# An adaLN transformer block on one core: four modulation sections as split 8-row matmuls, a new order around the first batch, and the last batch by tiles of tokens

## The reference

```python
mod = (silu(c) @ wmod).reshape(4, 6, 1, 512)             # c: 4 x 512, wmod: 512 x 3072
sa, ca, ga, sb, cb, gb = (mod[:, i] for i in range(6))
ga = (2 * (ga >= 0) - 1) * maximum(abs(ga), 0.25)        # gb alike
h = layernorm(x) * (1 + ca) + sa
x = x + ga * attention(h, Wqkv, bqkv, Wo, bo)            # softmax(q k' / sqrt(128)) v Wo + bo
h = layernorm(x) * (1 + cb) + sb
# ffn: h W_up' + sum over the top-1 expert e of (h A_e') B_e'
x = x + gb * ffn(h, W_up, gate_w, expert_bias, lora_A, lora_B)
```

## Time and profile before

| | |
|---|---|
| time, median of 3 runs | 217.23 us (216.91 to 218.76) |
| profiled execution: its time, its span | 216.85 us, 215.1 us |
| TensorE busy | 202.5 us, 94% of the span |
| VectorE, ScalarE, GpSimd busy | 130.4, 85.2, 79.1 us |
| TensorE's mean granted clock | 0.929 of full speed |
| moved by DMA | 19.50 MB |

### The profile page before, as it was taken

The page is one execution under the profiler, slowest core; times in us unless marked ns, Lnnn a source line. Parts: engine busy times, 40 slices in busy tenths (PEclk is TensorE's granted clock), DMA queues, the critical chain, the costliest instruction groups (busy, mean ns, idle before and its releaser), DMA issues.

```text
span 215.1 us, 3039 instructions
## 1 busy us (share of the span) xinstructions
PE 202.5 (94%) x1087; PEld 171.1 (80%) x1087; DVE 130.4 (61%) x309; ACT 85.2 (40%) x152; POOL 79.1 (37%) x103
## 2 busy tenths in 40 slices
PE   7999996989999999999999999999999999939992
PEld 6898975878899997798788879888887987726881
DVE  3828043778597561768786567738666365944353
ACT  2142003491177302973454667322466611343010
POOL 3451100008745059004346990004695001580040
PEclk9988997699996955999999999999999999985999
DMA  5999663227005005022002230000221000121004
GB/s 180 368 345 396 155 196 104 95 67 227 0 3 195 0 5 195 0 70 78 5 2 98 105 90 3 0 0 3 98 111 35 0 3 2 38 93 65 0 34 164
DMA packets 12887, 19.50 MB, mean 91 GB/s; under 512 B 3352, under 2 KB 3864, under 8 KB 12872
## 3 DMA queue, kind: packets, MB, share of 16 engines
q1 hardware_dynamic: 12872, 19.31, 26.8%
HBM read 15.09 MB, written 4.21 MB: 90 GB/s over the span
## 4 chain that ended last, share of the span: by engine, by line
PE 44%; POOL 2%; DVE 2%; issue 1%; ACT 1%; POOLq 0%
PE bank L331 30%; PE bank L488 2%; PE bank L486 2%; PE bank L438 2%; PE bank L465 2%; PE bank L525 1%; POOL xs L1246 1%; PE bank L498 1%; PE bank L420 1%; PE bank L417 1%; PE bank L423 1%; PE bank L394 1%; POOL rstd L1231 1%; PE bank L507 1%; PE bank L430 0%
## 5 line engine op out<-in xcount | busy, mean ns | idle before, releaser
L331 PE MATMUL bank<-wup_lo,h2hi 128*128 128x512 f32 x64 | 26.5, 415 | 0.0
L1231 POOL TENSOR_TENSOR rstd<-var_eps,neg_half 128x1 f32<-128x1 f32 x16 | 8.8, 549 | 45.4 <-DVE var_eps L1017 45.4
L331 PE MATMUL bank<-wup_hi,h2hi 128*128 128x512 f32 x64 | 25.4, 397 | 0.0
L331 PE MATMUL bank<-wup_hi,h2lo 128*128 128x512 f32 x64 | 25.4, 397 | 0.0
L741 ACT ACTIVATE xn_p<-xs,shift,rstd 128x512 f32<-128x512 f32 x16 | 13.0, 815 | 31.0 <-POOL shift L1234 31.0
L1246 POOL TENSOR_TENSOR xs<-xs,f_gb 128x512 f32<-128x512 f32 x14 | 17.9, 1289 | 14.8 <-DVE f_gb L1065 14.8
L1223 POOL TENSOR_TENSOR xs<-xs,gabo 128x512 f32<-128x512 f32 x16 | 20.1, 1289 | 0.0
L331 PE MATMUL bank<-h1lo,wqkv_hi 128*128 128x512 f32 x48 | 19.8, 412 | 0.0
L1210 POOL TENSOR_TENSOR wo_ga<-wo_raw,ga_bc 128x512 f32<-128x512 f32 x4 | 5.2, 1292 | 39.4 <-DMA ga_bc<-gates_dram 39.4
L331 PE MATMUL bank<-h1hi,wqkv_lo 128*128 128x512 f32 x48 | 19.0, 396 | 0.0
L331 PE MATMUL bank<-h1hi,wqkv_hi 128*128 128x512 f32 x48 | 19.0, 395 | 0.0
(11 more groups left out here) (164 smaller groups left out, 443.7 us busy)
## 6 DMA issues: line engine op xcount, KB each, us to landing
out_dram<-xs SPq DMA_DIRECT2D x16, 256.0 KB, 2.0
xs<-in_L_attn_x_dram SPq DMA_DIRECT2D x3, 1024.0 KB, 5.3
xs<-in_L_wmod_dram SPq DMA_DIRECT2D x3, 1024.0 KB, 5.2
xs<-in_L_attn_x_dram SPq DMA_DIRECT2D x4, 256.0 KB, 3.4
stage<-in_L_wmod_dram SPq DMA_DIRECT2D x4, 256.0 KB, 4.9
xs<-in_L_wmod_dram SPq DMA_DIRECT2D x4, 256.0 KB, 5.7
stage<-in_L_wmod_dram SPq DMA_DIRECT2D x1, 1024.0 KB, 13.2
ga_bc<-gates_dram SPq DMA_DIRECT2D x4, 256.0 KB, 3.9
```

Of the source, the lines that this page charges most:

```text
L331: mm = nc.tensor.matmul(dst, w, m, start=first and i == 0, stop=last and i == total - 1)
L1231: nc.gpsimd.tensor_tensor(rstd[:, 1, t:t + 1], var_eps[:, 1, t:t + 1], neg_half[:, 0:1], ALU.pow).then_inc(S["ln2_rstd"], 1)
```

## The change

Sections ga, sb, cb and gb (`ROWS`) are made by `mod_rows`: silu(c) is split in two parts of four columns, together the weights of 8 columns, and the section's high and low parts are streamed, 512 columns at a time, in 8 matmuls; the result is 8 rows. ScalarE splits off the high parts (`mod_high`), GpSimd the low ones (`mod_low`), but VectorE those of k = 1 and 3 of cb. ScalarE brings the rows out of PSUM (`mod_row_evacuate`), four small transposes (`mod_columns`) turn them into columns, and a reduction on VectorE (`section`) adds the two parts. Sections ca and sa keep the old form.

The order changes: ca's matmuls stand further ahead between the first transposes; the shift of q and k (`qkv_shift_columns`), the gate's and LoRA's transposes and sb's section stand earlier, `p_transposes(0)` ahead of `x1_transposes(1)`. Tiles 1 and 2 of the former are written into the banks of gateA and loraB. On SyncE the load of W_up moves ahead of the gate's write and read, and x2 and x3 wait until cb and gb are split. VectorE takes the first two statistics of x2 ahead of `residual(0, 0)`. In the last batch layer norm 2, x2T, h2's parts and `up` go by tiles of 128 tokens, and the third output tile is added by GpSimd in place of VectorE.

```diff
 
-SEQ = ("ca", "sa", "ga", "cb", "sb", "gb")
+
+COLUMNS = ("ca", "sa")
+ROWS = ("ga", "sb", "cb", "gb")
 SECTION = {"sa": 0, "ca": 1, "ga": 2, "sb": 3, "cb": 4, "gb": 5}
-GATE_STEPS = 4
+CB_BY_VECTOR = (1, 3)
+GATE_STEPS = 3
...
+        mod_split = {"ga": (phi, plo), "sb": (h2hi, h2lo), "cb": (wup_hi, wup_lo), "gb": (phi, plo)}
...
+                if of[0] in ROWS:
+                    return "mod_row_ready", ROWS.index(of[0]) + 1
+                return {"ca": ("modT_ready", 1), "sa": ("sa_split_ready", 2)}[of[0]]
+            if kind == "modT":
+                return "mod_sum_ready", ROWS.index(of[0]) + 1
...
+        def lows(s, kt):
+
+            n = ROWS.index(s)
+            by_vector = [NK * ROWS.index("cb") + k for k in CB_BY_VECTOR if NK * ROWS.index("cb") + k < NK * n + kt]
+            return NK * n + kt - len(by_vector), len(by_vector)
...
+            def wait_split(s):
+                sp.wait_ge(S["mod_hi"], NK * (ROWS.index(s) + 1))
+                by_pool, by_vector = lows(s, NK)
+                sp.wait_ge(S["mod_lo"], by_pool)
+                if by_vector:
+                    sp.wait_ge(S["mod_lo_dve"], by_vector)
...
-            wait_used("sa")
+            sp.wait_ge(S["mod_psum"], 2)
             sp.dma_start(raw["cb"], wmod_v[SECTION["cb"]]).then_inc(mod_in["cb"], 16)
-            wait_used("ga")
+            wait_split("ga")
             sp.dma_start(raw["gb"], wmod_v[SECTION["gb"]]).then_inc(mod_in["gb"], 16)
+            sp.wait_ge(S["x1T_psum"], 2 * NK)
+            sp.dma_start(raw["wup"][:], wup.rearrange("(o p) h -> p o h", p=P)).then_inc(wup_in, 16)
             write_gate(0)
             spread_gate(0, 0)
             spread_gate(0, 1)
-            sp.wait_ge(S["x1T_psum"], 2 * NK)
-            sp.dma_start(raw["wup"][:], wup.rearrange("(o p) h -> p o h", p=P)).then_inc(wup_in, 16)
-            wait_used("cb")
...
-            wait_used("gb")
+            wait_split("gb")
...
+            def mod_rows(s):
+
+                n = ROWS.index(s)
+                dst = open_bank("mod", s)
+                if n == 0:
+                    pe.wait_ge(S["silu_hi"], 1)
+                    pe.wait_ge(S["silu_lo"], 1)
+                for kt in range(NK):
+                    by_pool, by_vector = lows(s, kt + 1)
+                    pe.wait_ge(S["mod_hi"], NK * n + kt + 1)
+                    pe.wait_ge(S["mod_lo"], by_pool)
+                    if by_vector:
+                        pe.wait_ge(S["mod_lo_dve"], by_vector)
+                    w_hi, w_lo = (part[:, kt, :] for part in mod_split[s])
+                    both = silu_split[:, kt].rearrange("p a b -> p (a b)")
+                    nc.tensor.matmul(dst[0:2 * B, :], both, w_lo, start=kt == 0, stop=False)
+                    nc.tensor.matmul(dst[0:2 * B, :], both, w_hi, start=False,
+                                     stop=kt == NK - 1).then_inc(S["mod_kt"], 1)
+
+            def mod_columns(s):
+                n = ROWS.index(s)
+                dst = open_bank("modT", s)
+                pe.wait_ge(S["mod_row_ready"], n + 1)
+                for kt in range(NK):
+                    mm = nc.tensor.transpose(dst[:, kt * 2 * B:(kt + 1) * 2 * B], mod_row[:, n % 2, kt * P:(kt + 1) * P],
+                                             ident[0:2 * B, 0:2 * B])
+                mm.then_inc(S["modT_psum"], 1)
...
+            def last_x2_transposes(t):
+
+                dst = open_bank("x2T", LAST, t)
+                pe.wait_ge(S["xn2_ready"], NT * LAST + t + 1)
+                for kt in range(NK):
+                    mm = nc.tensor.transpose(dst[:, kt * P:(kt + 1) * P], xn2_p[:, t, kt * P:(kt + 1) * P], ident[:])
+                mm.then_inc(S["x2T_psum"], 1)
...
             qkv_shift_rows()
-            modulation("ga")
+            mod_rows("ga")
             qkv_shift_columns()
+            gate_transposes()
+            lora_b_transposes()
+            mod_columns("ga")
             scores(0)
             v_transposes(0)
+            mod_rows("sb")
             gate_to_rows("ga")
+            p_transposes(0)
             x1_transposes(1)
-            p_transposes(0)
+            pv(0)
+            mod_columns("sb")
             qkv(1, (0, 1))
-            pv(0)
-            qkv(1, (2,))
             out_projection(0)
-            qkv(1, (3,))
-            modulation("cb")
+            qkv(1, (2, 3))
+            mod_rows("cb")
             w_up_transposes(range(NK))
+            mod_columns("cb")
             x2_transposes(0)
-            modulation("sb")
-            gate_transposes()
-            lora_b_transposes()
-            modulation("gb")
+            mod_rows("gb")
             ffn_shift()
+            mod_columns("gb")
             gate_and_lora_a(0)
...
+                if last:
+                    last_x2_transposes(0)
+                    up(b - 1, 3, (0, 1))
+                    last_x2_transposes(1)
+                    up(b - 1, 3, (2, 3))
+                else:
+                    up(b - 1, 3)
...
-            last_x2_transposes()
+            last_x2_transposes(2)
+            up(b, 0)
+            last_x2_transposes(3)
+            up(b, 1, (0, 1))
             gate_and_lora_a(b)
-            up(b, 0)
+            up(b, 1, (2, 3))
             z_to_tokens(b)
-            up(b, 1)
+            up(b, 2)
             z_transposes(b)
-            up(b, 2, (0, 1))
+            up(b, 3, (0,))
             lora_up(b, 0)
             lora_up(b, 1)
-            up(b, 2, (2, 3))
+            up(b, 3, (1,))
             lora_up(b, 2)
-            up(b, 3)
+            up(b, 3, (2, 3))
             lora_up(b, 3)
...
+            def mod_high(s):
+                n = ROWS.index(s)
+                act.wait_ge(mod_in[s], 16)
+                if s == "gb":
+                    act.wait_ge(S["O_psum"], 1)
+                for kt in range(NK):
+                    nc.scalar.activation(mod_split[s][0][:, kt, :], raw[s][:, kt, :], ACT.Copy).then_inc(S["mod_hi"], 1)
+
+            def mod_row_evacuate(s):
+                n = ROWS.index(s)
+                act.wait_ge(S["mod_kt"], NK * (n + 1))
+                if n >= 2:
+                    act.wait_ge(S["modT_psum"], n - 1)
+                nc.scalar.activation(mod_row[:, n % 2, :], at("mod", s)[0:2 * B, :], ACT.Copy).then_inc(S["mod_row_ready"], 1)
...
+            def last_h2_high(t):
+                q = slice(t * P, (t + 1) * P)
+                act.wait_ge(S["x2T_psum"], NK * LAST + t + 1)
+                act.wait_ge(S["F_psum"], NT * (LAST - 1) + t + 1)
+                for kt in range(NK):
+                    nc.scalar.activation(h2hi[:, kt, q], at("x2T", LAST, t)[:, kt * P:(kt + 1) * P], ACT.Copy,
+                                         scale=modT["cb"][:, kt, LAST:B]).then_inc(S["h2_hi"], 1)
...
             gate_rows_evacuate("ga")
-            h1_high(1)
-            pt_high(0)
-            wo_high(0)
-            o_high(0)
-            ln2_normalise(0, (0,))
-            qkv_evacuate(1)
-            ln2_normalise(0, (1, 2, 3))
-            wup_high(range(NK))
-            h2_high(0)
             act.wait_ge(S["gateA_psum"], 1)
             nc.scalar.activation(gzw[:, :, 0, :], at("gateA")[:, 0:NK * GZ].rearrange("p (k g) -> p k g", k=NK),
                                  ACT.Copy).then_inc(S["gzw_hi_ready"], 1)
             act.wait_ge(S["loraB_psum"], 1)
             nc.scalar.activation(lbw[0:ZROWS, :], at("loraB")[0:ZROWS, :], ACT.Copy).then_inc(S["lb_hi_ready"], 1)
+            mod_row_evacuate("sb")
+            pt_high(0)
+            h1_high(1)
+            mod_high("cb")
+            wo_high(0)
+            o_high(0)
+            mod_high("gb")
+            ln2_normalise(0, (0, 1, 2))
+            qkv_evacuate(1)
+            ln2_normalise(0, (3,))
+            mod_row_evacuate("cb")
+            wup_high(range(NK))
+            h2_high(0)
             wo_high(1)
...
+                if s in COLUMNS:
+                    dve.wait_ge(S["mod_psum"], COLUMNS.index(s) + 1)
+                    return at("mod", s)[:, 0:NK * B]
+                n = ROWS.index(s)
+                dve.wait_ge(S["modT_psum"], n + 1)
+                nc.vector.tensor_reduce(mod_sum[:, n].rearrange("p (k b) -> p k b", k=NK),
+                                        at("modT", s)[:, 0:NK * 2 * B].rearrange("p (k a b) -> p k b a", k=NK, a=2),
+                                        AX_X, ALU.add).then_inc(S["mod_sum_ready"], 1)
+                dve.wait_ge(S["mod_sum_ready"], n + 1)
+                return mod_sum[:, n]
+
+            def mod_low(s, kts):
+                n = ROWS.index(s)
+                for kt in kts:
+                    dve.wait_ge(S["mod_hi"], NK * n + kt + 1)
+                    nc.vector.tensor_tensor(mod_split[s][1][:, kt, :], raw[s][:, kt, :],
+                                            mod_split[s][0][:, kt, :].bitcast(F32), ALU.subtract).then_inc(S["mod_lo_dve"], 1)
...
+            mod_low("cb", CB_BY_VECTOR)
+            inverse_sums(0)
```

(34 more changed lines are left out.)

182 lines of the change are left out of this document (99 added, 83 removed), and 6 rows, old and new, of the table order.

## The result

The changed kernel takes 222.57 us (median of 4, 222.5 to 222.7), the kernel before 217.07 beside it; the ratio is 1.0237, 95% interval 1.0185 to 1.0289, so it is slower by two to three per cent. The forecast was 217.9 with a range up to 221.4: the sign of the change was not called, and the time lies above the range. The profiled execution took 222.50 us with a span of 220.8; the forecast had a span of 215.8.

The account below looks back on a forecast made before the run. TensorE was taken as busiest, with each end decided by its last wait. Span 215.1 + 4.5 (first batch) + 0 (middle) - 3.8 (tail) = 215.8, giving 217.9 us as time; range 213.8 to 221.4.

Parts of the forecast that it names:

- The term that decides: First batch's end: gate's write waits behind W_up's megabyte, `wo_ga` 5.3 us later; queues put batch 1's scores +4.5 us.
- the rival in which the write passes: SyncE's queue: gate's write passes W_up's megabyte, everything behind 2.4 to 2.6 us sooner, 215.4 us; chance 0.17.
- The first batch up to the W_up load: Start of kernel: ga's section ends 2.1 us sooner, q, k shift at 32.2, scores at 34.5, x1T done at 45.5.
- The splits do not hold this up: First batch: ScalarE and idle GpSimd finish ga's low parts near 28, sb's near 33, wanted at 30.4 and 38.
- The slower clock rival: Batch 0's end at half clock, adding 4 instead of 2.1; earlier drop delays x1T up to 1.7; 219.8 to 221.5; chance 0.20.
- Moving ca forward: First batch: moving ca's matmuls forward gains 0.2 us (0 to 0.5), with eight warming matmuls between it and qkv.
- The gain rival: First batch: x2 and gate arrive in time, TensorE alone counts; about 199 us, or 207 with half; chance 0.11.
- The middle: Between the two ends the work stays the same: change 0, with 0.5 us either way.
- Sections: New sections on TensorE: 8 matmuls at 0.23 us, 1.85, plus 0.45 for transposes: 2.3 us against 4.0 before.
- The last batch: Tail by tiles: TensorE's end 4.9 us sooner, last store issued near 208.9 instead of 212.6; -3.8 us (-2.5 to -4.9).

Follow-up runs that it names:

- e1: Changed kernel with the first gate's write and its two reads put back ahead of the W_up load on SyncE; 214.16 us, ratio 0.977 to the kernel before.
- e5: Changed kernel with the first gate's write and two spreading reads issued by ScalarE instead of SyncE; 219.59 us, ratio 1.007 to the kernel before.
- e12: Changed kernel with GpSimd's low parts of sb made to wait, two for q and k's shift, two for the gate's columns; 218.37 us, ratio 1.007.
- e6: Changed kernel with 24 extra unused matmuls on TensorE in the gap ahead of LoRA's transposes; 223.77 us, ratio 1.026 to the kernel before.
- e14: Changed kernel with 10 extra unused matmuls on TensorE in the gap ahead of LoRA's transposes; 220.68 us, ratio 1.019 to the kernel before.
- e7: The changed kernel measured once more, nothing altered; 222.43 us, ratio 1.023 to the kernel before.
- e3: Changed kernel with both orders put back: gate's write ahead of W_up's load, x2's statistics behind the residuals; 210.25 us, ratio 0.960.
- e13: Changed kernel, both orders put back, cb split early, sb's low parts late, two x2 statistics ahead of q, k low parts, third output sum by VectorE; 201.10 us.
- e8: Changed kernel with the last batch put back to its old form, measured again beside the changed kernel; 224.10 us, ratio 1.029 to the kernel before.
- e2: Changed kernel with VectorE's first two statistics of x2 put back behind the four residuals; 216.46 us, ratio 0.988 to the kernel before.
- e4: Changed kernel with the last batch put back to its old form, first measurement; 224.59 us, ratio 1.023 to the kernel before.
- e9: On top of e3, cb's high parts split by ScalarE ahead of batch 0's softmax, all four low parts by GpSimd there; 208.37 us, ratio 0.964.

## Why the prediction was wrong, step by step

The span came out 5.0 us above its forecast: 3.1 up to the scores of batch 1, 0.7 in the middle and 1.2 in the last batch. Each has its step.

- **The term that decides** (W_up ahead of the gate's write) was right in mechanism and size. From W_up's issue to `wo_ga` 8.6 us were forecast and 8.6 measured; e1 and e5 show that it is the place in line, so the rival in which the write passes is out. From there every step kept its distance: `out_projection(0)` at 61.2 (58.2 forecast), x2's load 66.1 (63.1), the first residual 72.75 (69.8), scores of batch 1 at 94.6 (91.5). All are 3.0 to 3.1 us late, because x1T's end is: 48.7 for 45.5.
- **The step that failed** is in "The first batch up to the W_up load": "The splits do not hold this up". It asked whether TensorE would wait for GpSimd's low parts, and it doesn't. It did not ask what they do to VectorE, whose normalise and copies, 1.91 us and (in e12) 0.48 us with GpSimd idle, took 5.82 and 3.73 us beside them. Neither stands in any term of the sum, nor does the copies' new place ahead of the shift. q and k's shift stood on TensorE at 30.16, 2.0 us sooner than forecast, and the scores 0.6 us later than forecast: 2.6 us were lost between. e12 shows it: with sb's low parts out of the copies' way x1T ends at 44.9 in place of 48.7. The sign was in the trace of the kernel before, where the same copies took 2.96 us beside GpSimd.
- **The same part took full clock** for the scores, from a row of batch 1, though batch 0's own scores ran at 0.50. From the first score to x1T's end 11.0 us were forecast; at clock 1.00 it is 10.7 to 11.1 (e6, e12, e14), in the changed kernel it was 13.6 and 12.7 (e7). The slower clock rival named a drop at P's transposes, up to 1.7 us. It came earlier, behind the gap that VectorE made, and that part took 1.6 to 2.6 us longer. At the first batch's end the clock was priced right: from cb's columns at 83.69 to the scores of batch 1 it took 10.9 us, where 8.6 + 2.1 were forecast.
- **Moving ca forward** was priced at 0.2 us. ga's section started 2.4 us sooner (28.2 for 30.6), with the clock over 10 to 20 us at 1.00, where the kernel before has 0.83. The same kernel's second run (e7) has 0.83 there too, and the section at 29.8. So 0.8 us is the order's, and 1.6 are the clock's, which differed between two runs of one kernel: luck, and of no use, since VectorE held the scores in both (35.1 and 35.6).
- **The gain rival** (x2 and the gate in time, 199 to 207) was given 0.11 as a state of this kernel. It was not this kernel's, but with the waits gone e3 and e13 reach 210 and 201, so that state exists.
- **The middle** was taken to keep its length. It grew by 0.7 us here, by 2.2 in e3 and 2.4 in e13, nearly all of it ahead of batch 0's `lora_up`: TensorE waits there for ScalarE's normalise of batch 2 (0.43 us in the changed kernel) and, in e3 and e13, for VectorE (0.40 and 0.71), which it did not in the kernel before. The late queues of the first batch reach past the scores of batch 1. **Sections**: 8 x 0.23 us as forecast.
- **The last batch** was over-sized: -3.8 forecast, -2.6 in the span from the same `lora_up` on (-1.7 of time in e8). The matmuls end 4.3 us sooner, where 4.9 was forecast. TensorE's waits there are 2.0 us in 190.0 to 215.3, no more than the forecast's 2.5, and the clock was 1.00, so the missing 0.6 is time in which TensorE was busy; no run splits it further. Behind the last matmul 2.6 us were forecast up to the last store, from GpSimd's row; it is 2.8, but for another reason: VectorE's own last sum takes 1.58 us beside GpSimd's third, and in e13, with two on GpSimd, 0.80.

The range failed with this: its upper bound let the clock or the sum err, never VectorE's durations beside a busy GpSimd. Without the 3.1 us the time would lie inside it. e12, where that step is mended, took 218.37 us, close to the 217.9, but in part by luck: its scores of batch 1 start 1.6 us sooner than forecast, and the rest of its span is 2.4 us longer.

## What to carry to other kernels

Before work is given to an idle engine, list what runs beside it on its neighbours, and whether the durations used were measured with that company: GpSimd's free 26 us were not free for VectorE. When a small transfer or an early statistic is moved, write down what stands behind it in the same queue; two such reorderings cost 12.3 us here (e3), more than the 8.2 us that TensorE was spared, and taking both back turned a loss of 2% into a gain of 4%. When a stall is removed, look for the next one at once: the expectation of e2 and e3 missed GpSimd's queue just as the prediction missed what GpSimd's work does to VectorE.

## What the runs showed of the hardware

- VectorE is held by GpSimd in some instructions and not in others. Normalise, SBUF to SBUF: 0.48 us each with GpSimd idle, 1.46 beside it. The copy of 128 x 128: 0.16 and 1.24. The sum of two SBUF tiles: 0.69 and 1.27 to 1.58. The residual, with one operand in PSUM, takes 0.75 in either case, and the statistics 0.69. 1.2 us is about one of GpSimd's own instructions (1.28), so VectorE seems to wait for one to end. The Trainium skill, "SBUF — State Buffer", "SBUF: two separate sides", says just this: the two share a port pair under an exclusive lock that is held for a whole instruction, taken by VectorE's fast modes and, against a GpSimd instruction that reads SBUF, by its instructions with two SBUF inputs. The traces agree in each of these five, by their operands; which mode VectorE ran in they do not show.
- On one queue a small write (8 KB) behind a megabyte took 4.8 us (changed kernel), and on another queue at the same moment 1.4 us (e5).
- The longer TensorE stood idle ahead of LoRA's transposes, the lower was its granted clock in 34.1 to 41.6:

| idle there | runs | clock |
|---|---|---|
| 2.7 to 4.1 us | changed kernel, e1, e2, e4, e8, e9 | 0.54 to 0.58 |
| 1.4 to 1.5 us | e3, e7 | 0.77 |
| none | e5, e6, e12, e13, e14 | 1.00 |

The first run and e7 are one kernel. How long the gap gets depends on when TensorE comes to it, and so on its clock in 10 to 20 us, which differs from run to run: at 1.00 the shift stands at 29.8 to 30.2, at 0.83 at 31.6 to 32.4, at 0.66 (e5) at 33.9. e13 has 1.00 in both stretches and no gap, so the later clock goes with the gap and not with the earlier clock.
